# A transformer tower on one Trainium2 core: V, the gate's logits and layer norm's scaling go from VectorE to ScalarE, and V's biases are added later

## The reference

```python
h = W_tok[x]                                        # gather, 4 x 512 rows of 256
n = (h - mean(h)) / sqrt(var(h) + 1e-5)
q, k, v = n @ Wq + bq, n @ Wk + bk, n @ Wv + bv
h = h + local_attention(q, k, v) @ Wo + bo          # window 128, the window before it too, causal
n = (h - mean(h)) / sqrt(var(h) + 1e-5)
q, k, v = split(n @ W_qkv + b_qkv)
gate = softmax(n @ W_gate + b_gate); combine = top 2 of gate, others 0
h = h + full_attention(q, k, v)
      + sum_e combine[e] * (n @ W_experts[e] + b_experts[e])
```

## Time and profile before

| | |
|---|---|
| median of 3 runs | 600.5 us (600.39 to 601.75) |
| the profiled execution, span | 600.7 us |
| granted TensorE clock, mean | 0.979 |

### The profile page before, as it was taken

How to read it: one execution, slowest core, us unless ns; L and a number is a source line. 1 busy time by engine, 2 the same in 40 slices (tenths; PEclk the granted TensorE clock), 3 DMA queues, 4 the chain that set the end, 5 groups by cost and what they waited for, 6 DMA issues and landing times.

```text
span 600.7 us, 9520 instructions
## 1 busy us (share of the span) xinstructions
PE 539.3 (90%) x3209; PEld 283.9 (47%) x3209; DVE 424.7 (71%) x941; ACT 285.8 (48%) x558; POOL 188.1 (31%) x257
## 2 busy tenths in 40 slices
PE   3968998989899899998888899989999999999996
PEld 2435554654565335334533456444545555544442
DVE  6757766667877895887678877656876566678841
ACT  0314454536544563676354343525565455444444
POOL 6444746223422600211243233202233331043201
PEclk9978999999999999999997899999999999999999
DMA  6364534222332343353235132403259667232311
GB/s 194 103 199 129 159 95 156 68 74 81 116 89 67 111 113 100 94 158 102 71 94 154 55 108 86 124 18 113 67 174 267 191 201 238 70 104 72 108 54 35
DMA packets 45151, 69.23 MB, mean 115 GB/s; under 512 B 9208, under 2 KB 38320, under 8 KB 42416
## 3 DMA queue, kind: packets, MB, share of 16 engines
q1 hardware_dynamic: 40672, 55.64, 31.5%
q0 software_dynamic: 4224, 12.59, 6.8%
q10 hardware_dynamic: 208, 0.40, 0.2%
HBM read 45.25 MB, written 23.07 MB: 114 GB/s over the span
## 4 chain that ended last, share of the span: by engine, by line
PE 67%; DVE 18%; issue 7%; DMA 3%; ACT 3%; POOL 1%; ACTq 0%; SPq 0%; DVEq 0%
PE OB L1593 12%; PE R L1473 10%; PE R L1368 9%; PE SC L1543 8%; PE ST L1566 7%; DVE neg_max L1048 5%; PE R L1383 4%; PE R L1459 4%; PE SC L1548 3%; PE ST L1572 2%; PE R L1419 2%; PE R L1487 2%; DVE neg_max L1056 2%; DMA QS<-shiftT 2%; PE SC L1553 2%
## 5 line engine op out<-in xcount | busy, mean ns | idle before, releaser
L1048 DVE TENSOR_REDUCE neg_max<-SC 128x1 f32<-128x512 f32 x256 | 170.8, 687 | 78.1 <-PE SC L1543 74.9
L909 ACT ACTIVATE prob<-ST 128x512 f32<-128x512 f32 x256 | 136.7, 598 | 123.9 <-PE ST L1566 118.7
L1593 PE MATMUL OB<-prob,VS 128*32 128x512 f32 (+2 forms) x1024 | 107.2, 491 | 0.1
L1543 PE MATMUL SC<-KS,QS 96*128 96x512 bf16 x256 | 97.6, 389 | 8.6 <-DVE neg_max L1048 6.6
L912 ACT ACTIVATE prob<-ST 128x512 f32<-128x512 f32 (+1 forms) x128 | 68.0, 543 | 68.2 <-PE ST L1572 67.9
L745 POOL TENSOR_SCALAR_AFFINE_SELECT prob<-prob 128x512 f32<-128x512 f32 x64 | 40.9, 639 | 131.1 <-ACT prob L912 131.0
L1566 PE MATMUL ST<-QS,KS 98*128 98x512 bf16 x256 | 77.5, 380 | 1.9 <-ACT prob L909 1.9
L1056 DVE TENSOR_REDUCE neg_max<-SC 128x2 f32<-128x512 f32 x64 | 44.1, 688 | 22.0 <-PE SC L1553 21.6
L1053 DVE TENSOR_REDUCE neg_max<-SC 128x1 f32<-128x128 f32 (+1 forms) x128 | 39.6, 351 | 25.8 <-PE SC L1553 25.5
L1548 PE MATMUL SC<-KS,QS 96*128 96x256 bf16 (+1 forms) x256 | 48.0, 270 | 6.2 <-DVE neg_max L1053 2.7
L1543 PEld LDWEIGHTS SC<-KS,QS 96*128 96x128 bf16 x256 | 24.8, 97 | 55.1 <-DVE neg_max L1048 35.9
(11 more groups left out here) (156 smaller groups left out, 765.1 us busy)
## 6 DMA issues: line engine op xcount, KB each, us to landing
scratch<-parts SPq DMA_DIRECT2D x96, 128.0 KB
QS<-scratch SPq DMA_DIRECT2D x42, 256.0 KB, 3.3
KS<-scratch SPq DMA_DIRECT2D x42, 256.0 KB, 3.9
x_sorted<-ys SPq DMA_DIRECT2D x24, 128.0 KB, 3.2
xs<-x_sorted SPq DMA_DIRECT2D x12, 256.0 KB
y_sorted<-ys SPq DMA_DIRECT2D x12, 256.0 KB
QS<-scratch SPq DMA_DIRECT2D x12, 128.0 KB, 2.6
w_exp<-in_L_ffn_W_experts SPq DMA_DIRECT2D x6, 256.0 KB, 3.3
```

Source lines behind the costliest of these rows:

```text
L909: act.activation(prob[:, u % 2, e, :], src[:, :], ACT.Exp, scale=SCALE).then_inc(s_prob, 1)
L1048: dve.tensor_reduce(own_max[:, i, head:head + 1], bank[:, :], AX.X, ALU.max, negate=True).then_inc(s_max, 1)
L1543: pe.matmul(bank[:, :], Q[0:SHIFT_ROW, head, i * P:(i + 1) * P], K[0:SHIFT_ROW, head, :], start=True, stop=True).then_inc(s_sc_ps, 1)
L1593: mm = pe.matmul(OB[VW * i:VW * (i + 1), columns], VS[s % 3][:, kt, v:v + VW], p_of, start=(kt == 0), stop=(kt == NT - 1), skip_group_chec ...
```

## The change

- `store_v` is ScalarE's, as a plain copy out of PSUM without a bias (8 of 128x512, 16 of 128x256). The logits are copied by ScalarE as well (16 of 128x8), and VectorE adds the gate's bias to all of a preparation's once (128x32).
- From preparation 2 on (the third), `norm_apply` is ScalarE's: identity with scale `rstd` and bias `offset`, and POOL makes `offset` = -mean * rstd (128x4) ahead of it. Preparations 0 and 1 keep it on VectorE.
- The local V's bias: a new PE job ("bo", 0, 0) in the second half slot of stage 0 multiplies `bv` (widened to 128 equal columns, one VectorE copy ahead of stage 0) by `w_o`, two matmuls, and VectorE adds it to `o_bias` (`complete_bo`). Since `o_bias` is complete only then, `add_bo` of sequences 0 and 1 goes from START's half slot 24 and stage 0's half slot 5 to stage 0's slots 5 to 12, one tile in each.
- The full V's bias is a ninth row beside the experts' biases (51 rows of bias parts in place of 48, and three columns of ones beside the combine weights).
- Since a job is put in at the start of stage 0, each later job has the other of the two R banks.

```diff
+BIAS_ROWS = E + 1
+STACK_ROWS = len(BIAS_PRODUCTS) * E + PARTS
+BO_SLOT = 5
 AO_STEP, WO_STEP = (2, 6), (8, 9)
-GATE_STEPS, DENSE_GATE_STEPS = 16, 12
+GATE_STEPS, DENSE_GATE_STEPS = 13, 9
...
+    if (s, t) == (0, 1):
+        jobs.append(("bo", 0, 0))
...
-            for dst, src in ((v_bias[LOCAL], bv), (o_bias, bo)):
-                sp.dma_start(dst[:, :], src.rearrange("(a n) -> a n", a=1).to_broadcast([P, D])).then_inc(s_w, 16)
+            sp.dma_start(o_bias[:, :], bo.rearrange("(a n) -> a n", a=1).to_broadcast([P, D])).then_inc(s_w, 16)
...
+                for a in range(PARTS):
+                    n = STACK_ROWS - PARTS + a
+                    sp.dma_start(bias_stack[n:n + 1, :], bias_parts[E:BIAS_ROWS, a, :]).then_inc(s_bias_stack, 16)
...
+                if p >= 2:
+                    pool.wait_ge(s_rstd, p + 1)
+                    pool.tensor_tensor(offset[:, :], neg_mean[:, :], rstd[:, :], ALU.mult).then_inc(s_offset, 1)
...
-            def add_bo(b):
-                pool.wait_ge(s_xn, at(STAGE[LOCAL, b], NT, NT))
-                for t in range(NT):
-                    pool.tensor_tensor(h[:, b * NT + t, :], h[:, b * NT + t, :], o_bias[:, :], ALU.add)\
-                        .then_inc(s_hb, 1)
+            def add_bo(n):
+                if n == 0:
+                    pool.wait_ge(s_bo, 1)
+                if n % NT == 0:
+                    pool.wait_ge(s_xn, at(STAGE[LOCAL, n // NT], NT, NT))
+                pool.tensor_tensor(h[:, n, :], h[:, n, :], o_bias[:, :], ALU.add).then_inc(s_hb, 1)
...
-                    if what == "local" and step == (24 if p == 0 else q_step(p)[3] + 4):
-                        add_bo(b)
+                    if what == "local" and p > 1 and step == q_step(p)[3] + 4:
+                        for t in range(NT):
+                            add_bo(b * NT + t)
...
+                    if s == 0 and BO_SLOT <= u < BO_SLOT + 2 * NT:
+                        add_bo(u - BO_SLOT)
...
+            def norm_apply(p, t):
+                kind, b = STAGES[p]
+                if t == 0:
+                    act.wait_ge(s_offset, p - 1)
+                    act.wait_ge(s_x_ps, at(p, NC, 0))
+                act.activation(xn_of(p)[:, t, :], h[:, b * NT + t, :], ACT.Identity, bias=offset[:, t:t + 1],
+                               scale=rstd[:, t:t + 1]).then_inc(s_xn, 1)
...
+            def store_v(p, j):
+                kind = STAGES[p][0]
+                act.wait_ge(s_v_ps, V_BEFORE[p] + j + 1)
+                if p == 0:
+                    act.wait_ge(s_ones, 5)
+                if p >= 3:
+                    act.wait_ge(s_pv, UNITS * (p - 2))
+                bank, tiles = bank_of(("v", p, j)), 1 if kind == FULL else 2
+                heads = VS[p % 3][:, tiles * j:tiles * (j + 1), 0:H * VSTRIDE].rearrange("p t (n v) -> p t n v", n=H)
+                act.copy(heads[:, :, :, 0:HD],
+                         bank[:, 0:tiles * D].rearrange("p (t n d) -> p t n d", t=tiles, n=H)).then_inc(s_v, 1)
+                if kind == FULL:
+                    if j == 0 and STAGES[p][1] > 0:
+                        act.wait_ge(s_gexp, STAGES[p][1])
+                    act.copy(logit[:, j, :], bank[:, D:D + E]).then_inc(s_logit, 1)
...
+                    if step in (3, 4) and p >= 2:
+                        norm_apply(p, 2 * (step - 3))
+                        norm_apply(p, 2 * (step - 3) + 1)
...
+                    for j, first in enumerate(v_step(p)):
+                        if step == first:
+                            store_v(p, j)
...
-            def store_v(p, j):
-                kind = STAGES[p][0]
-                dve.wait_ge(s_v_ps, V_BEFORE[p] + j + 1)
-                if p >= 3:
-                    dve.wait_ge(s_pv, UNITS * (p - 2))
-                bank, tiles = bank_of(("v", p, j)), 1 if kind == FULL else 2
-                heads = VS[p % 3][:, tiles * j:tiles * (j + 1), 0:H * VSTRIDE].rearrange("p t (n v) -> p t n v", n=H)
-                dve.tensor_tensor(heads[:, :, :, 0:HD],
-                                  bank[:, 0:tiles * D].rearrange("p (t n d) -> p t n d", t=tiles, n=H),
-                                  v_bias[kind][:, :].rearrange("p (o n d) -> p o n d", o=1, n=H)
-                                  .to_broadcast([P, tiles, H, HD]), ALU.add).then_inc(s_v, 1)
-                if kind == FULL:
-                    dve.tensor_tensor(logit[:, j, :], bank[:, D:D + E], gate_bias[:, :], ALU.add).then_inc(s_gs, 1)
+            def complete_bo():
+                dve.wait_ge(s_w, 16 * QK_LOADS)
+                dve.wait_ge(s_bo_ps, 1)
+                dve.tensor_tensor(o_bias[:, :], bank_of(("bo", 0, 0))[:, 0:D], o_bias[:, :], ALU.add).then_inc(s_bo, 1)
...
-                dve.wait_ge(s_gs, gate_step_no(b, NT))
-                gate_step(b, dve.tensor_reduce(neg_top[:, :], logit[:, :, :], AX.X, ALU.max, negate=True), 5)
+                dve.wait_ge(s_logit, at(b, NT, NT))
                 gate_step(b, dve.tensor_tensor(logit[:, :, :], logit[:, :, :],
-                                               neg_top[:, :].unsqueeze(2).to_broadcast([P, NT, E]), ALU.add), 6)
+                                               gate_bias[:, :].unsqueeze(1).to_broadcast([P, NT, E]), ALU.add), 1)
...
-                    if step in (3, 4):
+                    if step in (3, 4) and p < 2:
                         norm_apply(p, 2 * (step - 3))
                         norm_apply(p, 2 * (step - 3) + 1)
-                    for j, first in enumerate(v_step(p)):
-                        if step == first:
-                            store_v(p, j)
...
+            dve.tensor_copy(bv_wide, bv_cols[:, :].unsqueeze(2).to_broadcast([P, NC, P])).then_inc(s_bv, 1)
...
+            def project_bv():
+                bank = claim(("bo", 0, 0))
+                pe.wait_ge(s_bv, 1)
+                for c in range(NC):
+                    mm = pe.matmul(bank[:, 0:D], bv_wide[:, c, :], w_o[:, c, :], start=(c == 0), stop=(c == NC - 1))
+                mm.then_inc(s_bo_ps, 1)
```

More of the change, by code:

```diff
@@ L294, in tower @@
         qk_bias = [sb(f"qk_bias{k}", [P, 2, NC]) for k in (0, 1)]
-        v_bias = [sb(f"v_bias{k}", [P, D]) for k in (0, 1)]
+        bv_cols = sb("bv_cols", [P, NC])
+        bv_wide = xsT[1][:, 0:NC * P].rearrange("p (c m) -> p c m", c=NC)
         o_bias = sb("o_bias", [P, D])
@@ L318, in tower @@
         stats = sb("stats", [P, NT, 6])
-        mean = sb("mean", [P, NT])
+        neg_mean = sb("neg_mean", [P, NT])
+        offset = sb("offset", [P, NT])
         var = sb("var", [P, NT])
@@ L386, in tower @@
         s_rstd = sem("rstd")
+        s_offset = sem("offset")
         s_xn = sem("xn")
@@ L414, in tower @@
         s_norm = sem("group_normalised")
+        s_bv = sem("bv_widened")
+        s_bo_ps = sem("bv_projected")
+        s_bo = sem("bo_complete")
         s_hb = sem("bo_added")
@@ L419, in tower @@
         s_h2 = sem("h2")
+        s_logit = sem("logits")
         s_gs = sem("gate_steps")
@@ L935, in prep @@
                         turned = bank_of(("comb", b, 0))[:, :].bitcast(BF16)
-                        act.copy(combT[:, :], turned[0:len(BIAS_PRODUCTS) * E, 0:T]).then_inc(s_combT, 1)
+                        act.copy(combT[:, :], turned[0:STACK_ROWS, 0:T]).then_inc(s_combT, 1)
                 if what == "out":
@@ L996, in mean_var @@
                 dve.tensor_tensor(apart[:, :], mean_e, mean_o, ALU.subtract).then_inc(s_join, 1)
-                dve.tensor_tensor(mean[:, :], mean_e, mean_o, ALU.add).then_inc(s_join, 1)
+                if p > 2:
+                    dve.wait_ge(s_xn, at(p, NT, 0))
+                dve.tensor_tensor(neg_mean[:, :], mean_e, mean_o, ALU.add).then_inc(s_join, 1)
                 dve.tensor_tensor(var[:, :], sq_e, sq_o, ALU.add).then_inc(s_join, 1)
@@ L1001, in mean_var @@
                                          op0=ALU.mult, op1=ALU.mult).then_inc(s_join, 1)
-                dve.tensor_scalar(mean[:, :], mean[:, :], 0.5, None, ALU.mult).then_inc(s_mv, 1)
+                dve.tensor_scalar(neg_mean[:, :], neg_mean[:, :], -0.5, None, ALU.mult).then_inc(s_mv, 1)
                 dve.wait_ge(s_join, at(p, 4, 4))
@@ L1007, in norm_apply @@
             def norm_apply(p, t):
-                kind, b = STAGES[p]
+                b = STAGES[p][1]
                 if t == 0:
@@ L1012, in norm_apply @@
                         dve.wait_ge(s_x_ps, at(p, NC, 0))
-                dve.tensor_scalar(xn_of(p)[:, t, :], h[:, b * NT + t, :], mean[:, t:t + 1], rstd[:, t:t + 1],
-                                  ALU.subtract, ALU.mult).then_inc(s_xn, 1)
+                dve.tensor_scalar(xn_of(p)[:, t, :], h[:, b * NT + t, :], neg_mean[:, t:t + 1], rstd[:, t:t + 1],
+                                  ALU.add, ALU.mult).then_inc(s_xn, 1)
             def leave_rest(p, i):
@@ L1115, in gate_weights @@
                     dve.wait_ge(s_gexp, b + 1)
-                    gate_step(b, dve.tensor_reduce(gden[:, :], gexp[:, :, :], AX.X, ALU.add), 7)
```

(8 more changed lines are left out.)

52 lines of the change are left out of this document (29 added, 23 removed).

## The result

The changed kernel takes 595.96 us in the median of 6 runs (595.21 to 598.45), the kernel before 600.39 in 6 runs beside it (599.13 to 601.75): a ratio of 0.993, 95% interval 0.9904 to 0.9957. Forecast were 594.0 us and 588.5 to 601.0. Four executions stood far outside of all others (1307.44, 881.7 and 643.55 us of the kernels of experiments 3, 5 and 6, and 698.33 us of the kernel before); no median, spread or ratio here contains them.

The account below looks back on a forecast made before the run. PE was taken as the bound, busy 539.3 of 600.7 us, its idle time winnable. Terms +1.4 - 0.7 + 0 - 1.6 + 0 - 1.7 - 1.6 - 2.3 = -6.5 gave 594.0 us, range 588.5 to 601.0.

Parts of the forecast that it names:

- Waits for V: PE's 8.3 us of waits for V's evictions, in ten waits, would go but for under 2 us.
- Stage 1: Preparation 3: two PE waits for V, 2.3 us, go and V's matmuls start 0.7 late: net -1.6 us.
- stage 4: Preparation 6, laid out like preparation 3 with the same two waits for V: -1.6 us.
- stage 3: Preparation 5: a 1.01 us wait for V goes and norm_apply's move gives 0.7: -1.7 us.
- stage 5: Preparation 7: waits for V of 2.0 us go and norm_apply's move gives 0.3: -2.3 us.
- START +1.4: At START, preparation 0's V copies delay ACT's issue of KS's loads: 1.4 us lost, bounds 0.2 and 1.84.
- add_bo -0.7: In START, POOL's o_bias addition no longer stretches DVE's cast and subtraction: 0.7 us gained, bounds 0.4 and 0.9.
- Stage 0 level: At stage 0's start, the bo job's 1.2 us cancels DVE's relief: 0, bounds -1.2 and +1.2.
- norm_apply on ACT: Scaling in preparations 2 to 7, 0.53 us each on ACT; V's matmuls 0.7 late in preparation 3.
- the hold: Exponential behind norm_apply ends 3.3 us later, 1.0 slack, nothing lost; slower rival: 2.8 in four preparations, 605.2, chance 0.14.
- Preparation 4 (stage 2): 0.4 us of waits for V against the same norm_apply block: 0, bounds -0.5 and +0.5.
- Rows of contraction: 0: Bias-stack matmuls with 51 rows instead of 48, whose length does not depend on the row count: 0.

Follow-up runs that it names:

- experiments 3, 5 and 6: Changed kernel with V and logits back on VectorE (600.32 us); with first norm_apply pairs made twice (603.80); with V, logits and scaling all on VectorE (601.44).
- experiment 6: The changed kernel with V, logits and layer norm's scaling all back on VectorE, also called bias_only: 601.44 us, ratio 1.001 to the kernel before.
- Experiment 3: The changed kernel with all copies of V and of the logits back on VectorE, scaling still on ScalarE: 600.32 us, ratio 0.9992 to the kernel before.
- Experiment 2: The changed kernel with preparation 0's second V copy put behind ScalarE's issues of KS's loads: 593.63 us, ratio 0.9874 to the kernel before.
- experiments 1 and 2: Changed kernel with preparation 0's V copied by VectorE (593.63 us, ratio 0.9871); with its second copy behind ScalarE's issues of KS's loads (593.63 us, 0.9874).
- experiment 7, before_add_late: The kernel before with POOL's o_bias addition for sequences 0 and 1 spread over stage 0's slots 5 to 12: 598.82 us, ratio 0.9968.
- experiments 3 and 4: Changed kernel with V and logits back on VectorE (600.32 us, ratio 0.9992); with layer norm's scaling back on VectorE in all preparations (595.61 us, 0.9925).
- experiment 4: The changed kernel with layer norm's scaling on VectorE in all preparations, V and logits still on ScalarE: 595.61 us, ratio 0.9925 to the kernel before.
- v0_dve_norm57: The changed kernel with preparation 0's V on VectorE and scaling on ScalarE only in preparations 5 and 7: 589.64 us, ratio 0.9825; again 590.46, 0.9816.
- bias_only: The changed kernel with V, logits and layer norm's scaling all back on VectorE: 601.44 us, ratio 1.001 to the kernel before.

## Why the prediction was right, point by point

- **Waits for V: right, mechanism and size.** Forecast were 8.3 us of waits gone but for under 2; they are 0.6. Stage 1 gave 2.57 for V less 0.51 for the late x, 2.1 net against 1.6; stage 4 gave 2.5 against 1.6; stage 3 2.0 against 1.7; stage 5 2.6, of which 0.3 isn't the moved work's, so 2.3 against 2.3. Experiment 3 shows that this is the change's gain.
- **START +1.4: right in cause, lucky in size.** The first score moved from 33.92 to 35.27, 1.35. Experiment 2 shows the order as its cause. But the forecast put the issue up to 1.84 late and the transfer shorter than before; the last transfer began 1.05 late (30.03 for 28.98) and took 5.20 us where it had taken 4.89. The two misses cancel. The medians of experiments 1 and 2 are 2.3 lower, more than 1.35. The clock doesn't account for that difference (0.9765 and 0.9735 in the median, 0.9745 for the changed kernel), and it is within what the intervals leave open.
- **add_bo -0.7: right in START,** where PE's wait fell from 3.15 to 2.36, 0.8, which experiment 7 shows alone. "PE isn't waiting for a shift in most" put no term to the one where it is: 1.04 us at unit 12, as much as START gave.
- **Stage 0 level: too low a gain.** The bo job took 0.87, the stretch up to unit 2 gave 1.75: -0.9 where 0 was taken, inside the bounds. By experiments 3 and 4 the 1.75 doesn't add up from V and `norm_apply` as the forecast had it: either alone gives it.
- **norm_apply on ACT: the hold harmless as forecast, the loss right in one stage of two.** For x 0.7 was forecast in stages 1 and 4: stage 1 lost 0.5, stage 4 nothing. Preparation 4 (stage 2) lost 0.5 where 0 was taken. The held exponential cost PE no wait over 0.3 us. As a part of the change scaling on ACT brought nothing (experiment 4). The price was right: a pair in a row takes 1.08 to 1.09 us as in the rows of experiment 4, 0.54 each, and I had 0.53. The trace agrees with the Trainium skill's figures (ScalarE: Activation LUTs, What ACT_TABLE_LOAD costs), from which a pair is an estimated 0.585 + 0.49 = 1.08.
- **The Trainium skill's rule for add and multiply on VectorE** (ScalarE: Activation LUTs, Rules for kernel authors) rests on a figure for bf16 and doesn't carry over to this case: V in float32 took ACT 584 and 373 ns where DVE took 687 and 417 (688 and 416 without the addition).
- **Rows of contraction: 0, right.** The matmul with the bias stack takes 274 ns with 48 rows and with 51.
- **The sum: -6.5 forecast, -6.7 between the profiles,** but as a balance. Without the three stretches of the clock the listed places gave 9.2 us, 2.7 more than the forecast, among them two that no term had: POOL's additions beside a shift at unit 12 (+1.0, which the prediction named, at 0.4) and a wait of PE for QS of 1.61 us at unit 15 that was 0.35. The clock took back 2.5 between the profiles. That the sum comes so near is luck.
- **Between the medians only 4.4 came, and two steps can explain the 2 us by which 594.0 missed.** One is the base: "since the span stood 0.2 above the median" compared a span with a device time; the profiled execution stood 2 us above (602.5 - 6.5 = 596.0). The other is the clock, which had no term: 0.9745 where before had 0.980, worth 3.3 us. Together they are more than the miss, so they overlap, and how they share it isn't shown. The lower clock goes with V on ACT, over all kernels here: the four with V on DVE, the kernel before among them, had medians of 0.980 to 0.985, those with V on ACT of 0.9735 to 0.979 (0.966 with the doubled pairs, 0.982 with the added products). Why isn't settled. In START a long wait of PE favours a drop, but experiments 1 and 2 shortened that wait from 4.2 us to 1.25 and 1.99, and the median clock stayed; in stage 4 the profiles of all kernels have low stretches of 10 to 27 us, after waits of PE that are the same in the kernel before and the changed one.

## What to carry to other kernels

When a busy engine waits for the bank that an eviction empties, moving the eviction to an engine that comes to it sooner is worth that wait; moving other work off the same engine was worth nothing (8.4 us against 0 for about equal work here). When work is put into another engine's list, look at what that list issues behind it, DMAs above all: the order of a copy and three loads was worth 1.35 us at the first score and 2.3 between the medians. And work that needs a chain of small results (statistics, rstd, offset) blocks the engine that it is moved to, here for 9.3 us, of which PE felt 0.5 in two places.

## What the runs showed of the hardware

The runs of one kernel follow PE's granted clock: for v0_dve_norm57 587.8 to 588.1 us at 0.979 to 0.987 (three runs), and 593.1 at 0.972; for bias_only 597.6 at 0.985 and 606.5 at 0.971. A difference of 1% between kernels is as large as that, so single profiles can't carry it, while the matched starts of products can. By the mean clocks (0.979 and 0.973) the profile of before spends some 25 us at the lower of the two levels, half of full clock, and that of the changed kernel some 32. The drops mostly follow waits of PE of one to four us (START, 1.61 us before 104 us in the kernel before, 1.1 us twice in stage 4 in both kernels), but not each such wait is followed by one in each profile. And the time outside of the span is 1.7 to 1.8 us in the kernels before and before_add_late and mostly 1.9 to 2.2 in those that carry V's biases in the new way, 0.3 us that no profile shows.
